# Two graph layers on one core: 18 turns of the identity taken out of TensorE's pauses ahead of the root's first product

## The reference

```
# layer 0: two edge types, 286 features inside
h   = t5_layer_norm(x, ln_weight)
out = h @ W_root + bias
for r in range(2):                       # mean over the edges of type r
    out = out + segment_sum((h[src] @ W_rel[r]) * (type2 == r)) / max(cnt_r, 1)
x   = layernorm(x + x + elu(out) @ wo_weight)          # "x1"

# layer 1: eight edge types, 1024 features
u = x @ root + bias
for r in range(8):
    mean = segment_sum(x[src] * (type8 == r)) / max(cnt_r, 1)
    u = u + mean @ weight[r]
z = concat([u, x]) @ w_gate + b_gate
x = layernorm(x + tanh(u) * z + x * (1 - z))
```

## Time and profile before

| | |
|---|---|
| median of 3 executions | 834.55 us (834.42 to 834.63) |
| the profiled execution | 834.18 us |
| its span, first to last instruction | 832.4 us |
| mean granted TensorE clock over the span | 0.999 |
| TensorE matmul busy | 816.1 us, 98% |
| VectorE busy | 672.2 us, 81% |
| ScalarE busy | 443.5 us, 53% |

### The profile page before, as it was taken

The page is one execution under the profiler, slowest core; times in us unless marked ns, Lnnn a source line. Parts: engine busy times, 40 slices in busy tenths (PEclk is TensorE's granted clock), DMA queues, the critical chain, the costliest instruction groups (busy, mean ns, idle before and its releaser), DMA issues.

```text
span 832.4 us, 15910 instructions
## 1 busy us (share of the span) xinstructions
PE 816.1 (98%) x6324; PEld 586.0 (70%) x6324; DVE 672.2 (81%) x949; ACT 443.5 (53%) x621; POOL 14.6 (2%) x32
## 2 busy tenths in 40 slices
PE   7999999999999999999999999999999999999996
PEld 5566755468776867768678686786867868768544
DVE  8999798998977777677776777867678677788897
ACT  6888788267555355353553545625446254445711
POOL 1000000000000000000000000000000000000000
PEclk9999999999999999999999999999999999999999
DMA  9622658202220120211202102022020220305811
GB/s 317 115 38 27 216 173 196 102 4 99 103 102 33 70 102 1 101 48 53 101 0 101 66 34 101 0 101 85 16 101 0 101 100 3 128 1 152 202 51 73
DMA packets 60214, 71.06 MB, mean 85 GB/s; under 512 B 30692, under 2 KB 34400, under 8 KB 60173
## 3 DMA queue, kind: packets, MB, share of 16 engines
q1 hardware_dynamic: 59297, 69.64, 26.9%
q10 hardware_dynamic: 876, 0.85, 0.4%
HBM read 57.96 MB, written 5.18 MB: 76 GB/s over the span
## 4 chain that ended last, share of the span: by engine, by line
PE 89%; DVE 6%; ACT 3%; DMA 1%; issue 1%; SPq 0%; DVEq 0%
PE psP L1246 51%; PE psA L1317 21%; PE psP L1043 12%; PE psA L1024 2%; PE psP L996 1%; ACT cu_mem L706 1%; DVE p_mem L1549 1%; PE psP L1052 1%; DVE vec L1465 1%; ACT wsplit L739 1%; DVE p_mem L1548 1%; ACT wsplit L690 1%; ACT dump L617 1%; DMA stage<-in_src 0%; DVE cu_mem L1688 0%
## 5 line engine op out<-in xcount | busy, mean ns | idle before, releaser
L1246 PE MATMUL psP<-wsplit,xT 128*128 128x256 f16 x2592 | 294.6, 273 | 0.0
L1246 PEld LDWEIGHTS psP<-wsplit,xT 128*128 128x128 f16 x2592 | 253.6, 98 | 33.0
L1317 PE MATMUL psA<-p_mem,cu_mem 128*128 128x512 f16 x800 | 175.3, 379 | 0.0
L1246 PE MATMUL psP<-wsplit,x 128*128 128x256 f16 x1296 | 150.3, 273 | 0.0
L1317 PEld LDWEIGHTS psA<-p_mem,cu_mem 128*128 (+1 forms) x800 | 78.3, 98 | 90.9 <-DVE cu_mem L1818 0.2
L1246 PEld LDWEIGHTS psP<-wsplit,x 128*128 128x128 f16 x1296 | 126.8, 98 | 14.7
L1510 DVE SCALAR_TENSOR_TENSOR wsplit<-stage,sc,wsplit 128x1024 f16<-128x1024 f32 x90 | 114.7, 1279 | 27.0 <-ACT wsplit L701 27.0
L701 ACT ACTIVATE wsplit<-stage,sc 128x1024 f16<-128x1024 f32 x90 | 100.6, 1137 | 16.1 <-DVE sc L1385 10.5
L1818 DVE SCALAR_TENSOR_TENSOR cu_mem<-psA,coef,cu_mem 128x512 f32<-128x512 f32 x80 | 60.0, 750 | 31.5 <-PE psA L1317 30.1
L701 ACT ACTIVATE wsplit<-x,sc 128x1024 f16<-128x1024 f32 x54 | 61.7, 1144 | 42.0 <-PE psP L1246 31.1
L1510 DVE SCALAR_TENSOR_TENSOR wsplit<-x,sc,wsplit 128x1024 f16<-128x1024 f32 x54 | 69.2, 1282 | 10.2 <-ACT wsplit L701 9.8
(11 more groups left out here) (223 smaller groups left out, 797.2 us busy)
## 6 DMA issues: line engine op xcount, KB each, us to landing
stage<-in_L_gnn_weight SPq DMA_DIRECT2D x16, 2048.0 KB, 7.9
stage<-in_L_gnn_w_gate SPq DMA_DIRECT2D x4, 2048.0 KB, 8.2
x_home<-x SPq DMA_DIRECT2D x5, 512.0 KB, 3.0
x<-x_home SPq DMA_DIRECT2D x5, 512.0 KB, 6.9
x<-in_x SPq DMA_DIRECT2D x4, 512.0 KB, 8.2
xT<-in_L_gnn_root SPq DMA_DIRECT2D x1, 2048.0 KB, 9.2
stage<-in_L_gnn_root SPq DMA_DIRECT2D x1, 2048.0 KB, 7.9
out<-x SPq DMA_DIRECT2D x4, 512.0 KB
```

Of the source, the lines that this page charges most:

```text
L1246: last = nc.tensor.matmul(psP[:, bank, (col + tt) * FB:(col + tt + 1) * FB], lhs[tt](a, c), split_block(n, b)[:, c, :], start=(first and t ...
L1317: last = nc.tensor.matmul(psA[:, (NT * h + t) % 2, :], cnt8[:, r, s, t * P:(t + 1) * P], p_part[h][a][:, s, :], start=(s == 0 and a == 0), ...
```

## The change

All three calls of `stay_busy(6)` and the helper itself are taken out. The degrees keep their places: types 0 and 1 and then 2 and 3 ahead of `wo_product(4)`, type 4 behind it, types 5 to 7 behind `root_product(0)`. `idle_turns` stays.

```diff
@@ -1090,11 +1090,6 @@
                 for m in range(IDLERS[n]):
                     nc.tensor.transpose(psP[:, m % 2, 0:P], ident[:, :], ident[:, :])
 
-            def stay_busy(n):
-
-                for _ in range(n):
-                    nc.tensor.transpose(psC[:, P:2 * P], ident[:, :], ident[:, :])
-
             pe.wait_ge(lnw_loaded, 16)
             nc.tensor.transpose(psC[:, 0:DC], lnw[:, :], ident[0:DC, 0:DC]).then_inc(lnw_turned, 1)
             idle_turns(0)
@@ -1219,14 +1214,11 @@
             turn_y(4)
             wo_product(3)
             degrees8(0, 2)
-            stay_busy(6)
             degrees8(2, 4)
             wo_product(4)
             pe.wait_ge(wo_full, 2 * NT)
             pe.sem_inc(w_used, 1)
-            stay_busy(6)
             degrees8(4, 5)
-            stay_busy(6)
             root_product(0)
             degrees8(5, R1)
             for t in range(1, NT):
```

## The result

The changed kernel takes 836.52 us in the median of 12 executions (834.08 to 838.36), the kernel before 834.55 us in the median of 12 (834.01 to 835.73). The ratio is 1.0018, with a 95% interval of 1.001 to 1.0026: some 1.5 us slower, clear of no change, though by less than the 0.2% that I had named as the bound. The executions fall into two groups. Four are where the kernel before is (834.08, 834.37, 834.41, 834.74), and eight lie from 836.28 to 838.36. The profiled one is the slowest of them, 838.36 us with a span of 836.6 us, so it has to be read as an execution of the second group, and it is the only one of that group with a trace. Its mean granted clock is 0.994, against 0.999 in the profile before. Over all twelve it is 0.993 to 0.996 in these eight, 0.999 in three of the four others and 0.996 in the fourth (834.41).

A forecast was written before the change was run, and what follows sets the result against it. TensorE, busy without a gap from 123.20 to 826.00 us, was taken to bound the kernel. The forecast was 834.18 + 0 + 0 + 0 = 834.18, plus 0.37 to the median: 834.6 us, range 834.1 to 836.4.

The forecast's parts named there:

- What bounds the kernel: TensorE is busy without a gap from 123.20 to 826.00 us, so any delay there is a delay of the result.
- The turns' own time: Ahead of the root's first product, the 18 turns' 2.07 us of TensorE are covered by waits: worth 0.
- A: Ahead of the root's first product the turns only fill pauses: 834.6 us, own range 834.2 to 835.0, chance 0.60.
- The price of the clock: TensorE's clock doesn't fall in the pause ahead of the root's first product: 0 taken, 1.7 us kept for the range.
- rival B: The clock falls between 119.7 and 123.2 us, ahead of the root's first product: 835.8 to 836.3 us, chance 0.29.
- Its upper bound: If the clock falls just ahead of 123.20, the product's first 3.3 to 3.5 us run at 1.2 GHz: 1.7 us.
- C: The clock comes back late and all of `root_product(0)` runs at half speed: 5.17 us more, 839.7 us, chance 0.07.
- both readings: Ahead of the root's product, 2.55 us of pause or 3.49 us with degrees, set against 4.6 us without work.
- Tile 1's margin: Tile 1's DMAs land at about 127.9 us and are wanted at 130.25: 2.3 us to spare, not touched.

The follow-up runs named there:

- experiment 2: Against the kernel before, only the last twelve turns, behind `wo_product(4)`, taken out: 836.63 us against 834.71, ratio 1.0028.
- Experiment 4: Against the kernel before, no turns, and degrees of types 5 to 7 moved ahead of the root's product: 835.42 us against 834.71, ratio 1.001.
- experiment 1: Against the kernel before, only the first six turns, between the degrees, taken out: 834.58 us against 834.71, ratio 0.9998.
- experiment 5: Against the kernel before, the third group has 12 turns in place of 6: 834.92 us against 834.68, ratio 1.001.
- experiment 6: Against the kernel before, each group of six turns replaced by four float16 products of 384 columns: 834.75 us against 834.68, ratio 0.9999.
- experiment 10: Against the kernel before, only the third group of six turns stays, right ahead of the root's product: 834.84 us against 834.68, ratio 1.0002.
- experiment 11: Against the kernel before, only the second group of six turns stays, right behind `wo_product(4)`: 835.81 us against 834.68, ratio 1.0013.
- Kernel 9: Against the kernel before, all eight degree types ahead of the root, spread among products and fewer turns: 836.0 us against 834.68, ratio 1.0014.
- experiment 3: Against the kernel before, the third group has 16 turns in place of 6: 836.74 us against 834.71, ratio 1.0022.
- experiment 12: Against the kernel before, ten one-column matmuls added behind the third group of turns: 837.9 us against 834.82, ratio 1.0032.
- experiment 8: Against the kernel before, all degrees ahead of the root, twelve turns in two groups, second half of `wo_product(4)` last: 834.4 us against 834.68, ratio 1.0.

## Why the prediction was right and wrong

**What bounds the kernel: right.** Each delay at the root's first product comes out at the end. In the two profiles 1.50 + 2.70 us at 132.57 become 4.18 us of time. TensorE has nothing to make it up with.

**The turns' own time: right.** Taking them out moved nothing forward. The second half of `wo_product(4)` and the product kept their starts, less the shift of the whole execution, and the pause became 2.54 us where I had worked out 2.55. The four executions at 834.08 to 834.74 us are this case, A.

**The price of the clock: the step that failed.** The prediction put it as "I take 0, the end that the only fall in this trace is nearer to". The fall at the end of the span came 4.6 us after TensorE's last work, and I read this as what a fall needs. In the changed kernel the clock fell with one-column matmuls up to 122.0 us and nothing for 1.3 us more. One fall gives one duration, not a bound. So the term for the clock, put at 0, was the wrong one: in the profiled execution the fall cost 2.70 us. A, with a chance of 0.60, was the case of 4 executions in 12. In the other eight the times and mean clocks fit rival B's mechanism, which one trace shows, at B's price or more.

**Its upper bound was too low.** I took 1.7 us, from 3.3 us of turns at the start. That was one rise, as the fall was one fall: in the changed kernel's profile all 20 of these first turns, from 4.7 to 9.2 us, stay at the lower level (at least 421 ns each), and the clock rises at 14.1. Measured in the product: 1.67 us in experiment 2, and 2.70 in the changed kernel's profile, where the clock came back 5.4 us after the product had begun, with 1.3 us of its 6.8 us at the lower level ahead of the product. That lies between B and C. By the ratio the time is 834.55 x 1.0018 = 836.1, inside the range of 834.1 to 836.4; the plain median of 836.52 is just above it. That the ratio's figure falls inside is owed to B at the range's end, not to the forecast of 0.

**The pause alone, or what fills it?** Experiment 4 gives the answer: with one-column matmuls up to the product's start the clock falls too. The prediction had both readings, 2.55 us of pause and 3.49 us "with the degrees in it", and found each shorter than 4.6 us. The second was the right stretch and the comparison was not: in the changed kernel the last matmul with wide columns ends at 120.87 + 0.38 = 121.25 us and the clock falls at 123.35, after 2.1 us in which 0.62 us were one-column matmuls. Even ahead of `wo_product(4)`, where I had looked for no fall at all, the clock falls at times behind the one-column matmuls (profiles of experiments 1, 2, 4, 5, 6, 10 and 11). It costs nothing as long as the wait behind it is longer than the delay: in experiment 5 it wasn't.

**Tile 1's margin: wrong, and without effect here.** The prediction took 2.3 us, from the start of the first of the two issues and one duration. The second DMA can only be issued when VectorE's low part is ready, 125.43 + 1.19 = 126.62 us, and lands some 3.1 us later, at 129.7; the margin to 130.25 is about 0.5 us. Kernel 9 found it.

**What stays open.** Whether an execution falls into the group with the loss or not isn't settled by the program: the same code does both, and what decides it isn't shown. Of the rest of the spread one case is traced, the 1.50 us of the first 25 us above.

## What to carry to other kernels

Look at what TensorE does in a pause ahead of long products before calling filler useless: here turns or products with wide columns kept the clock for the product, those right ahead of it seemed to do most, and matmuls with one column kept the busy rows full and lost it. A fall costs only where TensorE is late for something, so look for the wait behind it before paying for a cure. And count the instructions of the filler as well as its time: 20 of them, 0.25 us, made this kernel about 2.7 us slower by the ratio, in the profile half through a late DMA that a fetch stood ahead of and half through the clock behind it.

## What the runs showed of the hardware that I had not expected

Three things.

The granted clock was back only 5.4 us after the product's start in the changed kernel (124.70 to 130.1), against 3.3 us of turns at the start of the kernel before and 3.4 us in experiment 2 (123.57 to 127.0).

A fetch of 16 KB of instructions that began at 122.73 or 122.88 us went with transposing DMAs of 4.93 and 4.77 us; where it began at 124.14 (before), 125.74 (changed) or 123.82 (experiment 5), the DMA that the product waited for took 3.1 us or so. In kernel 9 it began at 122.76 and the DMAs took 3.1 us all the same: there the transfer's last packet had started by 122.86, and none was left to start when the fetch's packet ended. So what has to meet is the fetch and the last packets, ten of them in experiment 3 and two in experiment 12. These packets end 1.0 to 1.3 us late and the landing is 1.7 to 1.9 us late; the rest is open. That the fetch is TensorE's is inferred from when it comes. In the eight profiles with no more TensorE instructions ahead of the product than before it starts 0.9 to 1.2 us behind the product's start, whether 0, 12, 24 or 36 instructions are gone; in the six with more (experiments 3, 4, 5, 8, 9 and 12) it starts ahead of the product.

And the turns, which do nothing for the result, are worth 1.5 us (all eighteen, ratio 1.0018) to 2.3 us (the last twelve, ratio 1.0028, with overlapping intervals).
